# Token lists in bf16 in the buffer of stored rows, two experts' weights loaded earlier, and another order of constants and fills, in a fused attention and mixture-of-experts kernel

## The chip, the cores and the metric

The kernel runs on one core of one Trainium2 chip. The metric is the device time of one execution in microseconds (us); lower is better. In the text PE is the matrix engine (PEld its weight loads), DVE the vector engine, ACT the scalar engine, POOL the GpSimd engine, and SP the engine that issues most DMAs.

## The reference

```
x = x + layernorm(attn(layernorm(x)))        # x: (4, 1024, 256) f32
x = x + layernorm(ffn(layernorm(x)))

attn(c):  Q, K, V = c@Wq, c@Wk, c@Wv         # 16 heads of 16
          alpha = softmax(Q K^T / 4)         # over all keys
          alpha = where(causal, alpha, 0)    # masked after the softmax
          return alpha @ V

ffn(x):   probs = softmax(x @ router_w)      # 8 experts
          w, idx = top_k(probs, 2); w /= sum(w)
          return sum over e of combine[:, e] * (gelu(x @ w_fc[e]) @ w_proj[e])   # 256 -> 1024 -> 256
```

## The kernel before

The program goes through four stages, each engine with an instruction stream of its own, written out by hand. Semaphores alone order the engines.

**Stage 1, about 0 to 118 us.** Eight chunks of 512 tokens are normalised (DVE), transposed (PE, L931) and projected to Q, K and V (PE, L943 and L952). Q and K are split in three bf16 parts and stored to DRAM. Before it, POOL writes all constants. PE transposes with the constant `ident`, which is finished at L646 behind all fills; ACT's square root for the first chunk (L790) stands behind a warm-up activation (L786) that reads `cst0`, a constant that POOL fills at L627. Three of the fills, at L623, put ones into rows 96 to 119 of the three slots `ks` that hold K: each is 24 partitions by 4096 bf16 elements.

**Stage 2, about 118 to 1008 us.** Attention in 16 groups of four heads.

**Stage 3, about 1008 to 1057 us: routing.** Tokens are in eight blocks `g` of four tiles of 128, taken in the order `ORDER` = 0, 1, 2, 3, 4, 5, 7, 6; step `i` handles block `ORDER[i]`. The normalised rows lie in `yx`. SP stores them to DRAM (`store_x2`, L560; semaphore `s_x2w[i]`), so that rows can be gathered for each expert later, and stores the two gates of each token (`store_gate`, L565). `choose(i)` (DVE) picks the two best experts, `count(i)` (PE) ranks the tokens of each expert, `place(i)` (DVE) computes each token's slot. `place` also writes into `yx` a one-hot list `lo1` of the slot within a tile (L1310), for which the rows there must have been stored; it waits for `s_x2w[i]`. The last two steps, `i` = 6 and 7, come after the attention is over.

Then DVE, ACT and PE invert the map from tokens to slots. There are 64 (token tile, choice) pairs, handled in 4 batches of 16, with two buffers `hi1` in `arena`. For each batch, `hot` (L1522) compares the column `colf` of each pair with 71 numbers (`iota_c`), `hot_v` (L1529) multiplies the result with a value `vtab`, ACT (L880) multiplies it with the partition number, and PE (L1130) runs 16 matmuls of 142 moving columns that add everything up in one bank. `hot` of batch q waits for PE's batch q-2. From the sums DVE makes `tok` (L1549 to L1555), the list of rows to gather.

**Stage 4, about 1057 to 1625 us.** 71 tiles of 128 token slots, each of one expert: gather (POOL, L751), transpose (PE, L1142), first product (L1153), gelu (ACT), second product (L1163), scale (DVE), scatter with addition (POOL, L759). DVE copies the expert's first weights to `w1` (`copy_w`, L1560). The second weights lie in `arena`, whose part for experts 4 and 5 holds `hi1` during stage 3: SP loads these two (L553) once the lists are done and the first two gathers have landed, then it stores `x1` to the output (L600). PE waits for all second weights (`s_wp`) between the first product of tile 0 and that of tile 1. At the end the sums are normalised and added to the output.

Of the kernel before, what the change touches and what calls it, by code (L numbers as in the profile page):

```python
# [5 lines left out]
def sandwich(nc, x_d, wq_d, wk_d, wv_d, router_d, wfc_d, wproj_d, out_d):  # L6
# [7 lines left out]
    P = 128  # L14
# [33 lines left out]
    with ctx:  # L48
# [3 lines left out]
        def sem(name):  # L52
# [21 lines left out]
        lo1 = yx[:, :, :].rearrange("p t d -> p (t d)").bitcast(BF16).rearrange("p (g w) -> p g w", g=TT // TPC)\  # L74
            [:, :, 0:TOPK * TPC * P].rearrange("p g (j t l) -> p g j t l", j=TOPK, l=P)
# [4 lines left out]
        assert HSL * HW3 <= 2 * WSTEP and NPR % PCE == 0  # L80
# [78 lines left out]
        vtab = sb("vtab", [P, TOPK, TT])  # L159
# [6 lines left out]
        colf = rt[:, 0:TOPK * TT].rearrange("p (j t) -> p j t", j=TOPK)  # L166
# [39 lines left out]
        s_const = sem("s_const")  # L206
        s_x = [sem("s_x0"), sem("s_x1")]
# [63 lines left out]
        s_lc = sem("s_lc")  # L271
        s_hi = sem("s_hi")
# [176 lines left out]
        NCONST = 26  # L449
# [33 lines left out]
        def _(sp):  # L483
# [100 lines left out]
            for c in range(4 * KC, 6 * KC):  # L584
                load_wfc(c)
            for i in range(6):
                store_gate(i)
            for i in range(6, G):
                store_x2(i)
            for i in range(6, G):  # L590
                store_gate(i)
            sp.wait_ge(s_inv, NPR // PCE)
            for s in range(2):
                sp.wait_ge(s_xs[s], 16)
            for e in (4, 5):
                load_wproj(e)
# [13 lines left out]
        def _(pool):  # L610
            pool.memset(ident[:, :], 0.0).then_inc(s_const, 1)
            pool.memset(lower[:, :], 1.0).then_inc(s_const, 1)
# [8 lines left out]
            pool.wait_ge(s_const, 8 + NSL)  # L621
            for u in range(NSL):
                pool.memset(ks[u][MROW:MROW + MR], 1.0).then_inc(s_const, 1)  # L623
            pool.wait_ge(s_const, 8 + 2 * NSL)
            pool.memset(vone[:, 0:DH], 0.0).then_inc(s_const, 1)
            pool.memset(vone[:, DH:VW], 1.0).then_inc(s_const, 1)
            pool.memset(cst0[:, :], 0.0).then_inc(s_zero, 1)  # L627
# [18 lines left out]
            pool.affine_select(out=ident[:, :], in_=ident[:, :], compare_op=ALU.not_equal, fill=1.0,  # L646
                               base=0, pattern=[[-1, P]], channel_multiplier=1).then_inc(s_ident, 1)
# [136 lines left out]
        def _(act):  # L784
# [137 lines left out]
        def _(pe):  # L922
# [188 lines left out]
            pe.wait_ge(s_const, NCONST)  # L1111
            groups(pe, body)
# [11 lines left out]
            for q in range(NPR // PCE):  # L1124
# [4 lines left out]
                for n in range(PCE):  # L1129
                    ins = nc.tensor.matmul(bk(7)[:, 0:2 * NT], lo1[:, (q * PCE + n) % TT // TPC, (q * PCE + n) // TT, (q * PCE + n) % TPC, :],  # L1130
                                           hi1[q % HSL][:, n, 0:2, :].rearrange("p v c -> p (v c)"),
                                           start=(q == 0 and n == 0), stop=(q * PCE + n == NPR - 1),
                                           skip_group_check=True)
# [24 lines left out]
            def second_product(t, s, off):  # L1158
                wait_pos(pe, s_yo, t - 1)
# [20 lines left out]
            pe.wait_ge(s_wp, 16 * E)  # L1180
# [12 lines left out]
        def _(dve):  # L1193
# [52 lines left out]

            stats_c(0, 0, 16)
# [39 lines left out]
            def place(i):  # L1287
# [19 lines left out]
                dve.wait_ge(s_x2w[i], 16)  # L1307
                dve.wait_ge(s_lo, 3 * i + 3)
                for j in range(TOPK):
                    ins = nc.vector.tensor_tensor(lo1[:, g, j, :, :], lof[:, j, tiles].unsqueeze(2).to_broadcast([P, TPC, P]),  # L1310
                                                  iota_l[:, :].unsqueeze(1).to_broadcast([P, TPC, P]), ALU.is_equal)
# [204 lines left out]
            colf_n = rt[:, 0:TOPK * TT]  # L1516
            vtab_n = vtab[:, :, :].rearrange("p j t -> p (j t)")

            def hot(q):

                wait_pos(dve, s_inv, q - HSL + 1)
                nc.vector.tensor_tensor(hi1[q % HSL][:, :, 2, :],  # L1522
                                        colf_n[:, q * PCE:(q + 1) * PCE].unsqueeze(2).to_broadcast([P, PCE, NT]),
                                        iota_c[:, :].unsqueeze(1).to_broadcast([P, PCE, NT]),
                                        ALU.is_equal).then_inc(s_hi, 1)

            def hot_v(q):
# [125 lines left out]
```

## Time and profile before

| | |
|---|---|
| time, median of 3 runs | 1622.24 us (1619.61, 1622.24, 1626.62) |
| the profiled execution: time | 1626.82 us |
| its span, first to last instruction | 1625.1 us |
| busy: PE, DVE, ACT, POOL | 90%, 63%, 47%, 38% |
| mean granted clock of PE | 0.946 |
| PE, first product of the experts (L1153) | 270.3 us busy, x2272 |
| DMA moved | 105.07 MB, mean 65 GB/s |

The span holds everything that an engine did; the profiled execution's own time is 1.7 us longer. A busy PE says little about where time could be won, because most of it are the matmuls of stages 2 and 4, which the change leaves alone. What matters here are two short stretches in which PE stands still or works in fits: the first 18 us and the stretch from about 1000 to 1074 us.

### The profile page before, as it was taken

How to read it: one execution, taken by the hardware profiler on the slowest of the kernel's cores; microseconds unless marked ns; L12 is line 12 of the kernel's file. 1: busy time of each engine (PE TensorE's matmuls, PEld its weight loads, DVE VectorE, ACT ScalarE, POOL GpSimd, SP SyncE). 2: the span in 40 equal slices, each digit the busy share in tenths (PEclk: the TensorE clock that was granted, in tenths of full speed). 3: DMA queues.
4: the chain of work that ended last, by engine and by line, in shares of the span. 5: the costliest groups of instructions: out<-in, count | busy, mean ns of one | idle time of the engine just before them, and what ended most of it. 6: DMA issues, size and time to landing. Idle time of an engine off the chain costs nothing.

```text
span 1625.1 us, 31177 instructions
## 1 busy us (share of the span) xinstructions
PE 1455.0 (90%) x9750; PEld 836.1 (51%) x9751; DVE 1026.3 (63%) x1770; ACT 771.8 (47%) x1650; POOL 612.1 (38%) x711
## 2 busy tenths in 40 slices
PE   5988999999999899989999986389999999999990
PEld 3551233333333233323333243289999999999980
DVE  4769777777888788878888977723323233233324
ACT  2330577777777677767777785211111111111114
POOL 5332334543444334533444432123333333333332
PEclk9995899999999999999999998589999999999995
DMA  3569122022220222022213153262222222222229
GB/s 113 172 164 276 40 40 40 10 31 40 40 40 8 35 40 40 15 27 40 40 23 70 53 182 142 45 183 34 39 33 38 39 33 39 34 37 39 32 30 210
DMA packets 87629, 105.07 MB, mean 65 GB/s; under 512 B 11648, under 2 KB 70912, under 8 KB 87520
## 3 DMA queue, kind: packets, MB, share of 16 engines
q1 hardware_dynamic: 69664, 80.80, 21.5%
q0 software_dynamic: 17856, 22.89, 8.9%
q8 instruction: 60, 0.98, 0.3%
q14 instruction: 49, 0.40, 0.1%
HBM read 64.70 MB, written 38.96 MB: 64 GB/s over the span
## 4 chain that ended last, share of the span: by engine, by line
PE 61%; DVE 15%; issue 13%; ACT 4%; POOL 3%; DMA 2%; DVEq 1%; SPq 0%; POOLq 0%; ACTq 0%
PE ps L1153 16%; PE ps L1163 15%; PE ps L1008 10%; DVE negmax L1443 9%; PE ps L980 8%; PE ps L1094 8%; ACT wfc L868 2%; POOL x L668 2%; PE ps L973 2%; PE ps L1081 1%; DVE x L1348 1%; PE ps L1142 1%; ACT wfc L911 1%; DVE wfc L1454 1%; DMA arena<-in_L_ffn_w_proj 1%
## 5 line engine op out<-in xcount | busy, mean ns | idle before, releaser
L1443 DVE TENSOR_REDUCE negmax<-ps 128x1 f32<-128x1024 f32 x512 | 605.9, 1216 | 123.8 <-PE ps L1094 121.3
L868 ACT ACTIVATE wfc<-ps 128x512 f32<-128x512 f32 x768 | 436.6, 595 | 171.2 <-PE ps L980 162.7
L889 ACT ACTIVATE yx<-ps 128x512 f32<-128x512 f32 x142 | 84.8, 597 | 440.6 <-PE ps L1153 440.6
L1153 PE MATMUL ps<-yx 128*128 128x128 f32 x2272 | 270.3, 278 | 4.1 <-DMA arena<-in_L_ffn_w_proj 3.4
L1153 PEld LDWEIGHTS ps<-yx 128*128 128x128 f32 x2272 | 269.7, 195 | 8.3 <-DMA arena<-in_L_ffn_w_proj 3.6
L1163 PE MATMUL ps<-arena,yx 128*128 x1136 | 256.8, 379 | 0.0
L731 POOL TENSOR_TENSOR wfc<-wfc,causal 128x512 f32<-128x512 f32 x128 | 162.6, 1270 | 249.6 <-ACT wfc L868 181.7
L1094 PE MATMUL ps<-arena 96*128 96x512 bf16 x704 | 231.5, 413 | 9.6 <-DVE negmax L1443 4.0
L759 POOL DMA_INDIRECT expert_out<-yx,rt x71 | 112.6, 1586 | 318.3 <-DVE yx L1576 315.3
L1163 PEld LDWEIGHTS ps<-arena,yx 128*128 128x128 f32 x1136 | 210.4, 190 | 25.7
L980 PE MATMUL ps<-arena 120*128 120x512 bf16 x528 | 203.3, 392 | 12.8 <-ACT wfc L868 0.4
L1564 DVE SCALAR_TENSOR_TENSOR rt<-yx,rt 128x1 f32 (+1 forms) x71 | 15.6, 219 | 233.7 <-PE ps L1142 233.7
L1008 PE MATMUL ps<-wfc 128*16 128x128 f32 (+4 forms) x2304 | 161.5, 382 | 0.1
L863 ACT ACTIVATE ps<-ps 128x512 f32<-128x512 f32 x256 | 149.6, 584 | 11.7 <-PE ps L973 3.7
L980 PEld LDWEIGHTS ps<-arena 120*128 120x128 bf16 x528 | 50.2, 97 | 184.9 <-ACT wfc L868 115.0
L1560 DVE COPY yx<-wfc 128x2048 f32 x71 | 87.1, 1227 | 37.9 <-issue 37.9
L1094 PEld LDWEIGHTS ps<-arena 96*128 96x128 bf16 x704 | 65.5, 101 | 78.6 <-DVE negmax L1443 42.2
L1008 PE MATMUL ps<-wfc,vone 128*17 128x128 f32 (+3 forms) x1024 | 95.6, 445 | 7.2 <-issue 6.4
L1008 PEld LDWEIGHTS ps<-wfc 128*17 128x17 f32 (+1 forms) x2304 | 60.4, 97 | 76.1 <-issue 51.7
L980 PE MATMUL ps<-wfc 120*128 120x512 bf16 x240 | 93.0, 388 | 7.1 <-ACT wfc L868 0.8
L698 POOL TENSOR_TENSOR mparts<-negmax,zero 128x8 bf16<-128x8 f32 x64 | 12.8, 200 | 225.7 <-DVE negmax L1443 134.5
L751 POOL DMA_INDIRECT yx<-expert_in,rt x71 | 72.0, 1014 | 63.9 <-DVE rt L1555 34.8
(177 smaller groups left out, 1364.7 us busy)
## 6 DMA issues: line engine op xcount, KB each, us to landing
arena<-qk_parts SPq DMA_DIRECT2D x132, 128.0 KB, 5.9
qk_parts<-x SPq DMA_DIRECT2D x32, 384.0 KB, 2.6
arena<-in_L_ffn_w_proj SPq DMA_DIRECT2D x8, 1024.0 KB, 8.6
wfc<-in_L_ffn_w_fc SPq DMA_DIRECT2D x16, 512.0 KB, 7.5
wfc<-qk_parts SPq DMA_DIRECT2D x60, 128.0 KB, 6.1
expert_out<-rt SPq DMA_DIRECT2D x3, 1408.0 KB, 12.0
yx<-in_L_attn_content SPq DMA_DIRECT2D x8, 512.0 KB, 3.9
x<-in_L_attn_content SPq DMA_DIRECT2D x1, 4096.0 KB, 25.5
```

Of the source, the lines that this page charges most:

```text
L731: pool.tensor_tensor(md_sb[b % NET], et_sb[b % NET][:, :, q:q + P], causal[:, :].unsqueeze(1).to_broadcast([P, GH, P]), ALU.mult).then_inc ...
L759: pool.indirect_dma_start(out=ys_d, in_=yslot[t % 2], in_offset=None, out_offset=bass.IndirectOffsetOnAxis(ap=tok[:, t:t + 1], axis=0), co ...
L863: nc.scalar.activation(bk(ebank(c, g)), bk(ebank(c, g)), ACT.Exp, accum_out=den_u[:, (u - back) % NSL, hl, i:i + 1]).then_inc(s_expB, 1)
L868: nc.scalar.activation(et_sb[b % NET][:, hl, :], bk(ebank(c, g)), ACT.Exp).then_inc(s_expB, 1)
L889: nc.scalar.activation(hidT[s][:, 4 * hf:4 * hf + 4, :], bk(1 + hf).rearrange("p (c t) -> p c t", c=4), ACT.Gelu).then_inc(s_ge, 1)
L980: nc.tensor.matmul(bk(ebank(c, g)), ks[v][0:MROW + MR, hl, i * P:(i + 1) * P], qs[v][0:MROW + MR, hl, hf * 512:(hf + 1) * 512], start=True ...
L1008: ins = nc.tensor.matmul(out[32 * hl:32 * hl + rows, q0:q1], lhs, rhs, start=(i == 0 and piece == 0 and n == 0), stop=False, skip_group_ch ...
L1094: ins = nc.tensor.matmul(bk(2 * (k % 2) + hf), qs[u][0:SROWS, hl, i * P:(i + 1) * P], ks[u][0:SROWS, hl, hf * 512:(hf + 1) * 512], start=T ...
L1153: ins = nc.tensor.matmul(bk(1 + hf)[:, c * P:(c + 1) * P], w1[s][:, kc * FF + (4 * hf + c) * P:kc * FF + (4 * hf + c + 1) * P], xsT[:, kc, :],
L1163: ins = nc.tensor.matmul(bk(5 + s)[:, 0:D], hidT[s][:, c, :], arena[:, ds(off + c * D, D)], start=(c == 0), stop=(c == FC - 1))
L1443: nc.vector.tensor_reduce(negmax[:, hl % 2, i:i + 1], ps[:, 2 * (k % 2):2 * (k % 2) + 2, :], AX.XY, ALU.max, negate=True).then_inc(s_max, 1)
L1560: nc.vector.tensor_copy(w1[s], wfc[:, ds(off, WSTEP)]).then_inc(s_w1, 1)
```

## The change

The change has four parts.

1. The lists. `lo1` is packed into the first half of `yx` (step `i` writes token tiles 2i and 2i+1, and waits for `s_x2w[i // 2]`); the two buffers `hi1` move from `arena` into the second half of `yx`, with a new constant `iota_cn` behind them, a bf16 table that POOL writes once the block there has been stored and transposed. `colf` and `vtab` become bf16, and the layout of a `hi1` buffer goes from (pair, variant, column) to (variant, column, pair). So all operands of `hot` and `hot_v` are bf16 with 16 neighbouring elements, and a PE matmul of the inversion reads its 142 columns 16 elements (32 bytes) apart. `hot` now waits for the stores of blocks in steps 4 to 7.
2. SP stores block 7 (step 6) ahead of the gates, loads the second weights of experts 4 and 5 directly behind it, and stores block 6 (step 7) between the gates.
3. PE waits for the second weights at the second product of tile 0, not ahead of the first product of tile 1.
4. The constants. POOL fills `cst0` and `ident` first and finishes `ident` at once. The three fills of `ks` go from POOL to DVE, ahead of its first instruction of stage 1, with a semaphore `s_ones` of their own.

```
-        lo1 = yx[...].rearrange("p (g w) -> p g w", g=TT // TPC)[:, :, 0:TOPK * TPC * P].rearrange("p g (j t l) -> ...")
-        hi1 = [arena[:, 4 * WSTEP + s * HW3:4 * WSTEP + (s + 1) * HW3].bitcast(BF16)
-               .rearrange("p (n v c) -> p n v c", v=3, c=NT) for s in range(HSL)]
+        yx_b = yx[:, :, :].rearrange("p t d -> p (t d)").bitcast(BF16)
+        LO1 = TOPK * TT * P
+        lo1 = yx_b[:, 0:LO1].rearrange("p (i j t l) -> p i j t l", i=TT // TPC, j=TOPK, l=P)
+        hi1 = [yx_b[:, LO1 + 2 * s * HW3:LO1 + 2 * (s + 1) * HW3].rearrange("p (v c n) -> p v c n", v=3, c=NT)
+               for s in range(HSL)]
+        iota_cn = yx_b[:, LO1 + 2 * HSL * HW3:LO1 + 2 * HSL * HW3 + NT * PCE].rearrange("p (c n) -> p c n", c=NT)
-        vtab = sb("vtab", [P, TOPK, TT])
+        vtab = sb("vtab", [P, TOPK, TT], BF16)
-        colf = rt[:, 0:TOPK * TT].rearrange("p (j t) -> p j t", j=TOPK)
+        colf = rt[:, 0:TOPK * TT // 2].bitcast(BF16).rearrange("p (j t) -> p j t", j=TOPK)
...
 SP
             for c in range(4 * KC, 6 * KC):
                 load_wfc(c)
+            store_x2(6)
+            for e in (4, 5):
+                load_wproj(e)
             for i in range(6):
                 store_gate(i)
-            for i in range(6, G):
-                store_x2(i)
+            store_x2(7)
             for i in range(6, G):
                 store_gate(i)
-            sp.wait_ge(s_inv, NPR // PCE)
-            for s in range(2):
-                sp.wait_ge(s_xs[s], 16)
-            for e in (4, 5):
-                load_wproj(e)
...
 POOL
+            pool.memset(cst0[:, :], 0.0).then_inc(s_zero, 1)
             pool.memset(ident[:, :], 0.0).then_inc(s_const, 1)
+            pool.wait_ge(s_const, 1)
+            pool.affine_select(out=ident[:, :], ...).then_inc(s_ident, 1)
...
-            for u in range(NSL):
-                pool.memset(ks[u][MROW:MROW + MR], 1.0).then_inc(s_const, 1)
...
+            pool.wait_ge(s_x2w[ORDER.index(G - 1)], 16)
+            pool.wait_ge(s_x2t, KC * (ORDER.index(G - 1) + 1))
+            pool.iota(iota_cn, [[P, NT], [0, PCE]], base=0, channel_multiplier=0,
+                      allow_small_or_imprecise_dtypes=True).then_inc(s_cn, 1)
...
 PE
-                                           hi1[q % HSL][:, n, 0:2, :].rearrange("p v c -> p (v c)"),
+                                           hi1[q % HSL][:, 0:2, :, n],
...
             def second_product(t, s, off):
+                if isinstance(t, int) and t == 0:
+                    pe.wait_ge(s_wp, 16 * E)
...
             step(0, 0, first=True)
-            pe.wait_ge(s_wp, 16 * E)
...
 DVE
+            for u in range(NSL):
+                nc.vector.memset(ks[u][MROW:MROW + MR], 1.0).then_inc(s_ones, 1)
             stats_c(0, 0, 16)
...
-                dve.wait_ge(s_x2w[i], 16)
+                dve.wait_ge(s_x2w[i // 2], 16)
...
             def hot(q):
+                if q < HSL:
+                    for i in ((4, 5), (6, 7))[q]:
+                        dve.wait_ge(s_x2w[i], 16)
+                if q == 0:
+                    dve.wait_ge(s_cn, 1)
                 wait_pos(dve, s_inv, q - HSL + 1)
-                nc.vector.tensor_tensor(hi1[q % HSL][:, :, 2, :],
-                                        colf_n[:, q * PCE:(q + 1) * PCE].unsqueeze(2).to_broadcast([P, PCE, NT]),
-                                        iota_c[:, :].unsqueeze(1).to_broadcast([P, PCE, NT]),
-                                        ALU.is_equal).then_inc(s_hi, 1)
+                nc.vector.tensor_tensor(hi1[q % HSL][:, 2],
+                                        colf_n[:, q * PCE:(q + 1) * PCE].unsqueeze(1).to_broadcast([P, NT, PCE]),
+                                        iota_cn, ALU.is_equal).then_inc(s_hi, 1)
```

In the order listings below the line numbers are those of each kernel's own text.

SP, the DMAs at the end of the attention and in stage 3; `in_L_ffn_w_fc` are the first weights, `in_L_ffn_w_proj` the second, `expert_in<-yx` the stored rows, `expert_in<-gate` the gates. Before:

```order
95 L542 DMA wfc<-in_L_ffn_w_fc 128x1024 x12
96 L565 DMA expert_in<-gate 128x4x2 x6
97 L560 DMA expert_in<-yx 128x4x256 x2
98 L565 DMA expert_in<-gate 128x4x2 x2
99 L553 DMA arena<-in_L_ffn_w_proj 128x8x256 x2
```

And after:

```order
95 L546 DMA wfc<-in_L_ffn_w_fc 128x1024 x12
96 L564 DMA expert_in<-yx 128x4x256
97 L557 DMA arena<-in_L_ffn_w_proj 128x8x256 x2
98 L569 DMA expert_in<-gate 128x4x2 x6
99 L564 DMA expert_in<-yx 128x4x256
100 L569 DMA expert_in<-gate 128x4x2 x2
```

One store of rows and the two weight loads moved ahead of the first six gates; the other store stayed behind them.

DVE, the start of the program. Before:

```order
1 L1192 UNCONDITIONAL_BRANCH
2 L1197 BN_STATS stats<-yx 128x6 x4
3 L1199 MEMSET pause 128x1
4 L1201 BN_AGGR mv<-stats 128x2 x4
5 L1203 TENSOR_SCALAR mv<-mv 128x4
```

And after; the fills named `arena` and `wfc` are the rows of ones of the three slots `ks`:

```order
1 L1197 UNCONDITIONAL_BRANCH
2 L1253 MEMSET arena 24x4096 x2
3 L1253 MEMSET wfc 24x4096
4 L1202 BN_STATS stats<-yx 128x6 x4
5 L1204 MEMSET pause 128x1
```

The three fills now stand ahead of the first statistics.

## Rows read from the trace of the kernel before

**Rows 1.** Timeline, 0 to 18 us: start, duration, instruction, idle time before it.
```profile
0.82 0.20 POOL L611 MEMSET ident<- 128x128 f32 x1 [0.29 <-POOLq L1642]
...
3.26 6.99 POOL L623 MEMSET arena<- 24x4096 bf16 x2
...
4.78 1.41 DVE L1197 BATCH_NORM_STATS2 stats<-yx 128x6 f32<-128x256 f32 x4 [4.64 <-DMA yx<-in_L_attn_content]
...
6.63 0.17 DVE L1203 TENSOR_SCALAR mv<-mv 128x4 f32<-128x4 f32 x1
...
13.98 0.20 ACT L786 ACTIVATE warm<-cst 128x1 f32<-128x1 f32 x1 [11.88 <-POOL mhalf L628]
14.09 0.19 ACT L790 ACTIVATE std<-mv 128x4 f32<-128x4 f32 x1
...
15.52 0.29 POOL L646 TENSOR_SCALAR_AFFINE_SELECT ident<-ident 128x128 f32<-128x128 f32 x1 [0.16 <-POOL iota_c L643]
...
16.10 1.94 PE L931 MATMUL ps<-ident,yx 128*128 128x128 f32 x8 [16.10 <-DVE yx L1209]
```

**Rows 2.** Timeline of DVE around its fill of 512 elements.
```profile
932.87 2.35 DVE L1443 TENSOR_REDUCE negmax<-ps 128x1 f32<-128x1024 f32 x2
935.40 0.48 DVE L1421 MEMSET ps<- 128x512 f32 x1 [0.18 <-DVE negmax L1443]
935.79 1.34 DVE L1326 BATCH_NORM_STATS2 stats<-yx 128x6 f32<-128x256 f32 x4
```

**Rows 3.** Timeline of DVE, 1010 to 1011 us: first parts of one `var_y`.
```profile
1010.50 0.18 DVE L1335 BATCH_NORM_AGGREGATE mv<-stats 128x2 f32<-128x6 f32 x1
1010.52 0.06 DVE L1333 MEMSET pause<- 128x1 f32 x1
```

**Rows 4.** Timeline of DVE, stage 3.
```profile
1020.19 0.17 DVE L1304 CAST lof<-loi 128x8 f32<-128x8 int32 x1
1025.20 1.29 DVE L1310 TENSOR_TENSOR yx<-lof,iota_l 128x512 bf16<-128x512 f32 x2 [4.83 <-DMA expert_in<-yx]
...
1026.90 0.18 DVE L1263 COPY rt<-ps 128x32 f32<-128x32 f32 x1
...
1036.01 2.59 DVE L1522 TENSOR_TENSOR arena<-rt,iota_c 128x1136 bf16<-128x1136 f32 x2
1038.52 2.59 DVE L1529 TENSOR_TENSOR arena<-arena,vtab 128x1136 bf16<-128x1136 bf16 x2
...
1049.45 0.23 DVE L1549 TENSOR_SCALAR rt<-ps 128x71 f32<-128x71 f32 x1 [0.85 <-PE ps L1130]
```

**Rows 5.** Timeline of PE, stage 3 and the first tiles of stage 4.
```profile
1023.50 0.61 PE L1048 MATMUL ps<-ident,rt 128*128 128x32 f32 x2 [0.48 <-ACT rt L836]
...
1040.00 3.94 PE L1130 MATMUL ps<-arena,yx 128*128 128x142 bf16 x32 [10.72 <-ACT arena L880]
...
1057.56 6.21 PE L1153 MATMUL ps<-yx 128*128 128x128 f32 x32 [0.74 <-DVE yx L1568]
...
1067.37 6.43 PE L1153 MATMUL ps<-yx 128*128 128x128 f32 x32 [3.38 <-DMA arena<-in_L_ffn_w_proj]
...
1077.31 3.73 PE L1153 MATMUL ps<-yx 128*128 128x128 f32 x32
```

**Rows 6.** Timeline of ACT, the lists.
```profile
1037.38 2.51 ACT L880 ACTIVATE arena<-arena,pcol 128x1136 bf16<-128x1136 bf16 x2 [8.91 <-DVE arena L1522]
```

**Rows 7.** Timeline of DVE, `copy_w` for tile 1.
```profile
1065.20 1.23 DVE L1560 COPY yx<-wfc 128x2048 f32 x1 [0.61 <-issue]
```

**Rows 8.** Timeline of SP, the issues ahead of the last stores.
```profile
1008.15 11.01 SPq L565 DMA_DIRECT2D expert_in<-gate  x6
1019.20 1.05 SPq L560 DMA_DIRECT2D expert_in<-yx  x2
...
1057.32 1.00 SPq L553 DMA_DIRECT2D arena<-in_L_ffn_w_proj  x2
```

**Rows 9.** Busy time by stretch: each engine, PE clock, DMA share, GB/s.
```profile
1066.00:1067.00 1.00, 0.00 (x0) 0.00 (x0) 0.42 (x1) 0.00 (x0) 0.54 (x1) 0.51 1.08 383
```

More of the change, by code:

```diff
@@ L73, in sandwich @@
         NPR = TOPK * TT
-        lo1 = yx[:, :, :].rearrange("p t d -> p (t d)").bitcast(BF16).rearrange("p (g w) -> p g w", g=TT // TPC)\
-            [:, :, 0:TOPK * TPC * P].rearrange("p g (j t l) -> p g j t l", j=TOPK, l=P)
         PCE, HSL = 16, 2
         HW3 = PCE * 3 * NT // 2
-        hi1 = [arena[:, 4 * WSTEP + s * HW3:4 * WSTEP + (s + 1) * HW3].bitcast(BF16)
-               .rearrange("p (n v c) -> p n v c", v=3, c=NT) for s in range(HSL)]
-        assert HSL * HW3 <= 2 * WSTEP and NPR % PCE == 0
+        yx_b = yx[:, :, :].rearrange("p t d -> p (t d)").bitcast(BF16)
[4 more added lines that the diff above has]
+        iota_cn = yx_b[:, LO1 + 2 * HSL * HW3:LO1 + 2 * HSL * HW3 + NT * PCE].rearrange("p (c n) -> p c n", c=NT)
+        assert LO1 + 2 * HSL * HW3 + NT * PCE <= 2 * TT * D and NPR % PCE == 0
         NET = 3
@@ L206, in sandwich @@
         s_const = sem("s_const")
+        s_ones = sem("s_ones")
         s_x = [sem("s_x0"), sem("s_x1")]
@@ L271, in sandwich @@
         s_lc = sem("s_lc")
+        s_cn = sem("s_cn")
         s_hi = sem("s_hi")
@@ L448, in sandwich @@
         CRT, CRP = 5, 2
-        NCONST = 26
+        NCONST = 23
         NZERO = 7
@@ L610, in _ @@
         def _(pool):
+            pool.memset(cst0[:, :], 0.0).then_inc(s_zero, 1)
             pool.memset(ident[:, :], 0.0).then_inc(s_const, 1)
+            pool.wait_ge(s_const, 1)
+            pool.affine_select(out=ident[:, :], in_=ident[:, :], compare_op=ALU.not_equal, fill=1.0,
+                               base=0, pattern=[[-1, P]], channel_multiplier=1).then_inc(s_ident, 1)
             pool.memset(lower[:, :], 1.0).then_inc(s_const, 1)
@@ L645, in _ @@
             pool.wait_ge(s_const, NCONST - 6)
-            pool.affine_select(out=ident[:, :], in_=ident[:, :], compare_op=ALU.not_equal, fill=1.0,
-                               base=0, pattern=[[-1, P]], channel_multiplier=1).then_inc(s_ident, 1)
             pool.affine_select(out=lower[:, :], in_=lower[:, :], compare_op=ALU.is_gt, fill=0.0,
@@ L879, in _ @@
                 act.wait_ge(s_hi, q + 1)
-                nc.scalar.activation(hi1[q % HSL][:, :, 0, :], hi1[q % HSL][:, :, 2, :], ACT.Copy,
+                nc.scalar.activation(hi1[q % HSL][:, 0], hi1[q % HSL][:, 2], ACT.Copy,
                                      scale=pcol[:, 0:1]).then_inc(s_hip, 1)
@@ L1111, in _ @@
             pe.wait_ge(s_const, NCONST)
+            pe.wait_ge(s_ones, NSL)
             groups(pe, body)
@@ L1129, in _ @@
                 for n in range(PCE):
-                    ins = nc.tensor.matmul(bk(7)[:, 0:2 * NT], lo1[:, (q * PCE + n) % TT // TPC, (q * PCE + n) // TT, (q * PCE + n) % TPC, :],
-                                           hi1[q % HSL][:, n, 0:2, :].rearrange("p v c -> p (v c)"),
+                    j, tt = divmod(q * PCE + n, TT)
+                    ins = nc.tensor.matmul(bk(7)[:, 0:2 * NT], lo1[:, ORDER.index(tt // TPC), j, tt % TPC, :],
+                                           hi1[q % HSL][:, 0:2, :, n],
                                            start=(q == 0 and n == 0), stop=(q * PCE + n == NPR - 1),
@@ L1306, in place @@
                     dve.wait_ge(s_zero, NZERO)
-                dve.wait_ge(s_x2w[i], 16)
+                dve.wait_ge(s_x2w[i // 2], 16)
                 dve.wait_ge(s_lo, 3 * i + 3)
                 for j in range(TOPK):
-                    ins = nc.vector.tensor_tensor(lo1[:, g, j, :, :], lof[:, j, tiles].unsqueeze(2).to_broadcast([P, TPC, P]),
+                    ins = nc.vector.tensor_tensor(lo1[:, i, j, :, :], lof[:, j, tiles].unsqueeze(2).to_broadcast([P, TPC, P]),
                                                   iota_l[:, :].unsqueeze(1).to_broadcast([P, TPC, P]), ALU.is_equal)
```

12 lines of the change are left out of this document (4 added, 8 removed).

## The prediction

> **What bounds the kernel now.** I read the share of busy time first, then the chain that ended last, then the timelines of the stretches that the change touches. For most of the span PE works without a pause, in attention and in the 71 expert tiles, and no edit reaches those matmuls. So the change can only move what stands in front of them: the start, the routing, and the hand-over to the first tiles.
>
> At the start PE begins at 16.10 us [rows 1]. Two things arrive together: the normalised rows (DVE L1209, the releaser named) and `ident`, whose last step runs at 15.52. The rows are late because ACT could only start at 13.98, after 11.88 us of waiting for a constant that POOL fills behind the fills of ones: the two in `arena` alone take 6.99 us, 3.5 each, and the third is alike. DVE had its variances at 6.63 + 0.17 = 6.80 and then stood still.
>
> In the routing DVE is the last to arrive almost everywhere. It waits 4.83 us for a store to land, from about 1020.4 to 1025.20, then works through to the lists, which take from 1036.01 to 1049.45 [rows 4]. In stage 4 PE waits 3.38 us at 1067.37 for the last second weights [rows 5].
>
> **1. The start.** POOL's three fills (10.5 us) leave the path; three DVE fills of 4096 elements come onto it, since the first statistics stand behind them in the same queue. The trace has no fill of SBUF of this size on DVE. Its nearest row has 512 elements: 0.48 us by its own duration, 0.39 us from its start to the next instruction's start at 935.79, and 0.57 us from the end of the instruction in front (932.87 + 2.35 = 935.22) [rows 2]. The start of such a row seems to be stamped late: the fill L1333 is issued ahead of all the L1335 and yet stands at 1010.52, behind the first of them at 1010.50 [rows 3]. So I take 0.57 less some 0.04 for the handing over, 0.53 us for 512 elements, or 1.04 ns each: 4.25 us for 4096, 12.8 for three. By 0.39 it would be 3.1 each and 9.4 in all; by 0.57, 13.7.
>
> The Trainium skill (VectorE: DVE Perf Modes, section Zero memsets can be issued as uint32 (trn2)) says that a memset takes one cycle per element whatever the type, so bf16 would not help here; by its clock of 0.96 GHz that is 12.8 us too. It is a rule against this edit.
>
> DVE can begin at about 0.8 us, as POOL does (0.82), so the fills end at 13.6. Then come 6.80 - 4.78 = 2.02 us of statistics, about 0.1 to ACT, and 16.10 - 14.09 = 2.01 us from ACT's root to PE: 17.8 against 16.10. `ident` and `cst0` are long ready, and POOL is free before its first task. **Term: +1.7 us** (13.7 us of fills: +2.6; 9.4: -1.7). If the fills took no time, the rows would be at hand at 4.78 and PE would start at 4.78 + 2.02 + 0.1 + 2.01 = 8.9: -7.2, the floor. Everything behind, up to the routing, shifts by the same.
>
> **2. The wait in step 6.** `place(6)` now waits for the store of step 3, long landed, so its list starts at about 1020.5 rather than 1025.20. But 4.7 us are not won: next is `choose(7)`, before at 1026.90, and it needs PE's logits, 1023.50 + 0.61 = 1024.11 [rows 4, 5]. PE's chain up to there doesn't depend on the removed wait. DVE is free at about 1022.2 and now waits for PE until 1024.2. **Term: 1026.90 - 1024.2 = -2.7 us.** What is late next is PE.
>
> **3. The lists.** Before, from the first `hot` to the use of the sums: 1049.45 - 1036.01 = 13.44 us. Two `hot` take 2.59 us, 1.34 each with 0.09 overlapping, and `hot_v` the same; two of ACT's copies 2.51; 32 matmuls 3.94, so 1.97 a batch and 123 ns a matmul [rows 4 to 6]. New: `hot` and `hot_v` with all operands bf16. The trace shows no such DVE instruction with two inputs; bounds are 1.34 (nothing gained) and, by the rate of L1560, 1.23 us for 2048 elements or 0.60 ns each [rows 7], 0.68. I take 0.75, near the latter: the operands now are as narrow and as regular as they can be. ACT's copy stays at 1.25, the number of elements is the same. PE's batch stays at 1.97, see below. From the new `hot` at 0: `hot` 0 ends at 0.75, `hot` 1 at 1.4, `hot_v` 0 at 2.05; ACT's first copy ends at 2.05, its second at 3.3. PE runs batch 0 from 2.2 to 4.2 and batch 1 to 6.1. `hot` 2 waits for batch 0 and ends at 5.1, ACT at 6.4; batch 2 runs from 6.5 to 8.5. `hot` 3 waits for batch 1, ends at 7.1, ACT at 8.4; batch 3 to 10.5; with 0.1 for the step to DVE 10.6. **Term: 10.6 - 13.4 = -2.8 us.** It isn't more because ACT and PE, not DVE, carry this chain now. Without any gain on DVE the term is 0.
>
> The new waits of `hot`: `s_cn` follows the store of step 6, which now is in front of the gates, and a table that POOL writes while idle; it is there by about 1023. The store of step 7 is issued behind six gates (11.01 us in all, from 1008.15 [rows 8]) and behind 2 MB of weights. Before, both stores had landed by about 1026. The weights add between 5.5 us (2.1 MB at the 383 GB/s of [rows 9]) and 10 (issued at 1057.32, landed at 1067.37 [rows 8, 5]): 1031.5 to 1036. `hot` 1 needs it at 1036.01 - 2.7 + 0.65 = 1033.95. Value 0, at worst +2. The stores of `x1` to the output, which now follow at once, are done before the first gather.
>
> **4. The second weights.** PE's wait of 3.38 us ends at 1067.37, but the first product of tile 1 also needs `copy_w`, which ends at 1065.20 + 1.23 = 1066.43 [rows 5, 7], and nothing here makes that earlier. **Term: 1066.5 - 1067.37 = -0.9 us.** What is late next is DVE's copy. The wait in its new place, at the second product, finds the weights there.
>
> **Reading 32 bytes apart.** No matmul of the trace reads its moving columns so. The nearest row that costs more per column is L1153: 128 f32 columns, 32 in 6.43 us, 201 ns or 1.57 ns a column against 0.87 for L1130 [rows 5]; at 1.57, 16 matmuls take 3.6 us and the lists 2.2 + 4 x 3.6 + 0.1 = 16.7, term +3.3 rather than -2.8. Value 1.97: PE's granted clock is at its lower level here (0.50 to 0.52), so that it asks for one column in 0.83 ns only. The Trainium skill (SBUF — State Buffer, section Door 1: The DMA port swizzle) says that SBUF works in lines of 16 bytes and that each access to a new line pays a penalty, up to a stride of 8 bf16 being free. Here every column would be a new line; it gives no price in time. By the rule the matmuls lengthen, and that is the third rival.
>
> **Sum.** +1.7 - 2.7 - 2.8 - 0.9 = -4.7 us. Against the profiled execution: 1626.8 - 4.7 = 1622.1. That execution is 4.6 us above the median of the runs (1622.24), as the same kernel's runs spread; so the median should be 1622.24 - 4.7 = **1617.5 us**.
>
> **The rivals.**
> - *Fast fills.* DVE fills bf16 in SBUF two or four elements a cycle: three in 6.4 or 3.2 us. PE starts at 11.4 or 8.9, the term is -4.7 or -7.2, the sum -11.1 to -13.6: 1608.6 to 1611.1. For it: DVE does 1.23 us for 2048 f32 in a copy [rows 7], so two a cycle exist. Against: the f32 row of [rows 2] shows one a cycle. Chance 0.18.
> - *The clock.* PE's first product of tile 1 took 6.43 us where a settled one takes 3.73 [rows 5]; the clock had fallen to its lower level by 1066.00 to 1067.00 (0.51) [rows 9], after PE had stood still since about 1064. It now starts at 1066.5 of that time, at the very edge. If the fall comes later it gains 2.7, and some 0.9 are in the last batch of the lists, as PE now pauses less between batches: sum about -8.3, 1613.9. Against: a pause of 2.5 us remains. Chance 0.14.
> - *The reading stride, the other side.* If a moving column 32 bytes from the last costs double, a batch takes 3.94 us, the lists 2.2 + 15.8 + 0.1 = 18.1, term +4.6, sum +2.7: 1624.9, slower. It decides from 202 ns a matmul (3.24 us a batch), where the term of the lists is +1.8 and the sum about 0. At 201 ns (the L1153 rate, or 1.6 x before) it just eats all. Chance 0.12.
> - *No gain from bf16 on DVE,* the change not doing what it says: the lists at 0, sum -1.9, 1620.3. Or the store of step 7 late by 2 us: 1619.5. Together 0.08.
> - The forecast: 0.48.
>
> **How the numbers follow.** A measurement of this kernel can tell some 0.5% (8.1 us) from no change, so faster means below 1614.1 and slower above 1630.4. Fast fills give faster nearly always (0.17); the clock case lies at the edge (0.08); from the forecast, with a shorter fill and the runs' own spread (7 us from lowest to highest), 0.07 more: 0.32. Slower: a stride that costs more than double, or a start or a store worse than bounded: 0.06. Same: 0.62. The range runs from 1608, which takes in nearly all of the fast fills, to 1625, the stride at double.
>
> **What the profile after would show.** The three fills on DVE from 0.8 us, and PE's first transpose at 17.8 (11.4 or 8.9 in the first rival). `choose(7)` waiting for PE, not for a DMA, at about 4.7 - 2.7 = 2 us. `hot` at 0.75 us. PE's batches of the lists in 1.97 us; at 3 or more the stride is to blame. From the first `hot` to L1559 10.6 us. PE's wait before tile 1 2.5 us, put down to DVE's copy. The forecast falls if fills run more than one element a cycle, if a `hot` still takes 1.34, or if the first product of a settled tile (3.73 us) changes at all.

## The result, and the profile after

The changed kernel takes 1627.73 us (median of 20 runs, 1625.10 to 1630.22) where the kernel before, on the same chip, takes 1623.72 (20 runs, 1619.61 to 1626.62). The ratio is 1.0024, 95% interval 1.0018 to 1.0031: 4.0 us slower (2.9 to 5.0 by the interval). I had forecast 1617.5, between 1608 and 1625. The forecast was wrong: a gain of 4.7 us turned into a loss of 4.0.

The profiled execution of the changed kernel took 1627.36 us, with a span of 1625.6 and a mean granted clock of 0.946. That of before had the same clock and a span of 1625.1, because it was one of the longer runs of its kernel (1626.8 against a median of 1623.7). So the two spans hide most of the difference, and stages are compared by their own length.

The start, as the timeline of the changed kernel shows it (start, duration, instruction, idle time before it):

```profile
1.73 3.47 DVE L1253 MEMSET arena<- 24x4096 bf16 x1 [1.58 <-PEq L1652]
6.00 3.47 DVE L1253 MEMSET arena<- 24x4096 bf16 x1 [0.80 <-issue]
10.27 3.47 DVE L1253 MEMSET wfc<- 24x4096 bf16 x1 [0.80 <-issue]
13.78 1.41 DVE L1202 BATCH_NORM_STATS2 stats<-yx 128x6 f32<-128x256 f32 x4
...
16.29 1.38 DVE L1214 TENSOR_SCALAR yx<-yx,mv,rstd 128x256 f32<-128x256 f32 x4
...
17.82 1.94 PE L933 MATMUL ps<-ident,yx 128*128 128x128 f32 x8 [17.82 <-DVE yx L1214]
```

From one fill's start to the next's are 4.27 us, though a row says 3.47: the missing 0.80 stands as "issue" in front of the next row. It fits the late start stamp that [rows 2, 3] hinted at, and the fills of half as many elements below bear it out. PE starts at 17.82 instead of 16.10 [rows 1]: +1.72, forecast +1.7.

Stage 3 on DVE, the timeline of the changed kernel. The stage begins at 1008.95 here and at 1009.05 before, so these times can be held against [rows 4] nearly as they are:

```profile
1020.73 1.29 DVE L1317 TENSOR_TENSOR yx<-lof,iota_l 128x512 bf16<-128x512 f32 x2 [0.46 <-DVE lof L1311]
...
1024.04 0.19 DVE L1270 COPY rt<-ps 128x32 f32<-128x32 f32 x1 [1.05 <-PE ps L1050]
...
1033.17 1.41 DVE L1534 TENSOR_TENSOR yx<-rt,yx 128x1136 bf16<-128x1136 bf16 x2
1034.50 1.41 DVE L1540 TENSOR_TENSOR yx<-yx,vtab 128x1136 bf16<-128x1136 bf16 x2
...
1039.77 0.75 DVE L1534 TENSOR_TENSOR yx<-rt,yx 128x1136 bf16<-128x1136 bf16 x1 [3.22 <-PE ps L1134]
...
1043.80 0.75 DVE L1534 TENSOR_TENSOR yx<-rt,yx 128x1136 bf16<-128x1136 bf16 x1 [2.50 <-PE ps L1134]
...
1052.02 0.23 DVE L1559 TENSOR_SCALAR rt<-ps 128x71 f32<-128x71 f32 x1 [5.60 <-PE ps L1134]
```

The wait for the store has gone: `place(6)` starts at 1020.73, and `choose(7)` waits for PE's logits and starts at 1024.04 instead of 1026.90, after 1.05 us of waiting for them (I had put this wait at 2). A `hot` takes 0.75 us instead of 1.34. But from then on DVE waits for PE again and again, 3.22, 2.50 and 5.60 us. The reason stands on PE, in its timeline of the changed kernel:

```profile
1023.40 0.60 PE L1050 MATMUL ps<-ident,rt 128*128 128x32 f32 x2 [0.47 <-ACT rt L838]
...
1035.39 16.60 PE L1134 MATMUL ps<-yx 128*128 128x142 bf16 x64 [8.94 <-DVE yx L1540]
...
1060.15 6.36 PE L1157 MATMUL ps<-yx 128*128 128x128 f32 x32 [0.74 <-DVE yx L1578]
...
1068.79 5.47 PE L1157 MATMUL ps<-yx 128*128 128x128 f32 x32 [2.06 <-DVE yx L1570]
...
1077.77 3.73 PE L1157 MATMUL ps<-yx 128*128 128x128 f32 x32
```

All 64 matmuls stand in one unbroken group of 16.60 us: 259 ns each, against 123 ns [rows 5]. PE never waits there any more, it is the bound. From the first `hot` to the use of the sums are 1052.02 - 1033.17 = 18.85 us, before 13.44. The second weights did move as meant: PE's wait ahead of tile 1 is now put down to DVE's copy and is 2.06 us instead of 3.38.

### The profile page after: what moved, and what is told of

It is laid out like the page before. It is cut to its first block, busy times and chain, and to the rows that moved or that the text cites. A ratio compares the mean times of both kernels' runs of the same rounds, so it can differ in the third digit from the quotient of the medians.

```text
span 1625.6 us, 31180 instructions
## 1 busy us (share of the span) xinstructions
PE 1459.6 (90%) x9750; PEld 835.8 (51%) x9751; DVE 1036.4 (64%) x1773; ACT 771.6 (47%) x1650; POOL 603.2 (37%) x709
## 4 chain that ended last, share of the span: by engine, by line
PE 62%; DVE 15%; issue 13%; ACT 4%; POOL 3%; DMA 1%; DVEq 1%; SPq 0%; POOLq 0%; ACTq 0%
PE ps L1157 16%; PE ps L1169 15%; PE ps L1010 10%; DVE negmax L1450 9%; PE ps L982 8%; PE ps L1096 7%; ACT wfc L870 2%; POOL x L666 2%; PE ps L975 2%; PE ps L1134 1%; DVE x L1355 1%; PE ps L1083 1%; PE ps L1146 1%; ACT wfc L913 1%; DVE wfc L1461 1%
## 5 line engine op out<-in xcount | busy, mean ns | idle before, releaser
L1586 DVE TENSOR_SCALAR yx<-ps,rt 128x256 f32<-128x256 f32 x71 | 34.3, 484 | 98.4 <-PE ps L1169 98.4
L696 POOL TENSOR_TENSOR mparts<-negmax,zero 128x8 bf16<-128x8 f32 x64 | 12.8, 200 | 226.1 <-DVE negmax L1450 134.8
```

## The experiments

Theory A, after the result: the moving columns of L1134, read at a stride of 32 bytes, make each matmul 136 ns longer and the lists 5.4 us longer; all other parts do what the forecast said. Theory B: something else slows these matmuls (the buffers that moved from `arena` to `yx`, the stores to the output beside them, or the low clock). A second question was whether the start could be had without DVE's 12.8 us.

Each kernel was timed against the kernel before on the same chip; "before" below is the median of those runs of it. Where two changed kernels are compared, each is first taken against its own "before". The profile rows of a section are from the kernel of its heading unless another is named.

### Only the stride added to the kernel before

```
-  .rearrange("p (n v c) -> p n v c", v=3, c=NT)     # columns of one n are neighbours
+  .rearrange("p (v c n) -> p v c n", v=3, c=NT)     # 32 bytes apart; buffers stay in arena, tables f32
```

> The kernel before with one edit: the order of elements in the list buffers is (variant, column, pair), the buffers stay in arena, colf and vtab stay f32, no DMA runs beside the lists. Theory A (the stride alone): a matmul takes 259 ns instead of 123, four batches 16.6 us on PE, the lists 20.7 us instead of 13.4 since the first batch starts as late as before; 7.3 us slower than the kernel before, about 1631 us (ratio 1.0045). Theory B (yx, bf16 or the DMAs beside): 123 ns, no difference.

Measured: 1631.54 us (before 1623.32), ratio 1.0053 (1.0039 to 1.0066). The timeline:

```profile
1032.13 2.59 DVE L1522 TENSOR_TENSOR arena<-rt,iota_c 128x1136 bf16<-128x1136 f32 x2
...
1036.12 16.60 PE L1130 MATMUL ps<-arena,yx 128*128 128x142 bf16 x64 [10.71 <-ACT arena L880]
...
1052.76 0.23 DVE L1549 TENSOR_SCALAR rt<-ps 128x71 f32<-128x71 f32 x1 [4.42 <-PE ps L1130]
```

The window over the lists (length, busy time of PE, PEld, DVE, ACT and POOL, then PE clock, DMA share and GB/s), and behind it one from the kernel before, at its own first batch:

```profile
1036.00:1053.00 17.00, 16.60 (x64) 7.94 (x64) 8.49 (x10) 3.98 (x5) 0.00 (x0) 0.50 0.00 0
```

```profile
1040.00:1041.00 1.00, 1.00 (x9) 1.00 (x10) 1.00 (x1) 0.00 (x0) 0.00 (x0) 0.50 0.00 0
```

The group has 16.60 us again, to the hundredth, with the buffers in `arena`, f32 tables and no DMA running (0 GB/s). The first `hot` stands at 1032.13, so the lists take 20.63 us, 7.2 more than before. This one edit costs 8.2 us. Theory A is shown, and B falls: of its three causes two are absent here, and the third, the low clock, is there with neighbouring columns too (0.50 in both windows), so it does not slow a matmul by itself. Whether the stride would cost anything at the higher clock is not shown.

### The changed kernel with the old order

```
-  hi1: .rearrange("p (v c n) -> p v c n")   hot, hot_v: [P, NT, PCE]   PE: hi1[..][:, 0:2, :, n]
+  hi1: .rearrange("p (n v c) -> p n v c")   hot, hot_v: [P, PCE, NT]   PE: hi1[..][:, n, 0:2, :]
   # hot reads the f32 constant iota_c again; POOL's table iota_cn and the wait for it are dropped
```

> The changed kernel with the old order of elements in the list buffers (pair, variant, column), so that a matmul of the inversion reads its 142 columns side by side; the buffers stay in yx and everything else stays as changed. Theory A (the stride: columns 32 bytes apart slow the moving reads): the 64 matmuls fall from 259 ns to some 123 ns each, a hot takes 1.34 us again, the lists take 13.4 us from the first hot to the use of the sums instead of 18.85; 5.4 us less than the changed kernel, about 1622.3 us, and about 2 us below the kernel before (ratio 0.9988). Theory B (what slows the matmuls is where and when they run: operands in yx, or the 4 MB of output stores that now run beside them): the matmuls stay at about 259 ns and the time at about 1627.7 us or more.

Measured: 1619.85 us (1619.11 to 1622.02; before 1623.03), ratio 0.998 (0.9971 to 0.9989). From its timeline, PE and then DVE:

```profile
1036.90 3.94 PE L1129 MATMUL ps<-yx 128*128 128x142 bf16 x32 [10.71 <-ACT yx L877]
...
1054.67 5.54 PE L1152 MATMUL ps<-yx 128*128 128x128 f32 x32 [0.74 <-DVE yx L1572]
...
1062.48 3.84 PE L1152 MATMUL ps<-yx 128*128 128x128 f32 x32 [2.06 <-DVE yx L1564]
```

```profile
1032.90 2.59 DVE L1527 TENSOR_TENSOR yx<-rt,iota_c 128x1136 bf16<-128x1136 bf16 x2
...
1035.41 2.59 DVE L1534 TENSOR_TENSOR yx<-yx,vtab 128x1136 bf16<-128x1136 bf16 x2
...
1046.58 0.23 DVE L1553 TENSOR_SCALAR rt<-ps 128x71 f32<-128x71 f32 x1 [1.10 <-PE ps L1129]
```

The matmuls are back at 123 ns in `yx`, which takes the place of the buffers out of theory B as well. `hot` and `hot_v` are back at 1.33 to 1.35 us each. `hot` reads `iota_c`, which is f32, but every operand of `hot_v` (L1534) is bf16 and it gains nothing either: in this order its second input repeats one element 71 times at the innermost level. The other way round, `hot_v` of the kernel with only the stride added is regular but has an f32 table, and takes 1.34 us. So DVE's gain needs the narrow type and the regular order, and it is that order which makes PE step 32 bytes. The lists take 13.68 us, and the other parts of the change gain 0.2% by themselves. The time is 3.2 us below that of before (1.8 to 4.7), so 7.2 below the changed kernel's. By the profiles the lists account for 5.2 of it, and the first products of the first two tiles, 5.54 and 3.84 us against 6.36 and 5.47, for another 2.5. Those two come from the clock: in the first tile it rose earlier, and ahead of the second it did not fall. Two windows of this kernel, over the pause ahead of the second tile's product, and in a fence of its own two of the changed kernel:

```profile
1061.00:1062.00 1.00, 0.00 (x0) 0.00 (x0) 0.82 (x2) 0.00 (x0) 0.71 (x1) 1.00 0.00 0
1062.00:1063.00 1.00, 0.52 (x4) 0.52 (x5) 0.43 (x1) 0.00 (x0) 1.00 (x1) 1.00 0.00 0
```

```profile
1068.00:1069.00 1.00, 0.21 (x1) 0.21 (x2) 0.73 (x1) 0.00 (x0) 1.00 (x1) 0.96 0.00 0
1069.00:1070.00 1.00, 1.00 (x6) 1.00 (x6) 0.00 (x0) 0.00 (x0) 0.55 (x1) 0.50 0.00 0
```

The pause is 2.06 us in both. Why the clock fell in the one and not in the other is open.

### How far apart is too far

```
-  PCE, HSL = 16, 2
+  PCE, HSL = 8, 2      # columns 16 bytes apart, 8 batches     (second kernel: 4, 2: 8 bytes, 16 batches)
   # POOL writes its table iota_cn only behind the stores of steps 4 to 7
```

> The changed kernel with batches of 8 pairs: the columns of a matmul lie 16 bytes apart instead of 32. If each column in a new 16-byte line costs the same, a matmul stays at 259 ns; if the cost grows with the distance, it falls to some 190 ns.

> The changed kernel with batches of 4 pairs: columns 8 bytes apart, two of them in each 16 bytes. If two hits per 16-byte line are enough for the full rate, a matmul takes 123 ns; if any distance above neighbouring costs, 259 ns or between.

Measured, one run each, so that the rows say more than the times: 1629.36 us at 16 bytes and 1619.91 at 8. The timeline at 16 bytes, then two batches of four matmuls at 8:

```profile
1037.82 16.32 PE L1135 MATMUL ps<-yx 128*128 128x142 bf16 x64 [9.07 <-ACT yx L883]
```

```profile
1039.34 1.24 PE L1135 MATMUL ps<-yx 128*128 128x142 bf16 x8 [0.40 <-ACT yx L883]
```

At 16 bytes a matmul takes 255 ns, as at 32. At 8 bytes the four matmuls of a batch start 0.11 to 0.13 us apart, about as with neighbouring columns (0.12). So the step lies between 8 and 16 bytes, and from 16 to 32 bytes the price hardly grows. Only powers of two were tried, so a step by 16-byte lines is not told apart here from another cause that sets in at a stride of 16. The Trainium skill (SBUF — State Buffer, section Door 1: The DMA port swizzle) says two things on this: that a line has 16 bytes and wants at least two hits to run at full rate, with which the three groups agree (two hits a line at 8 bytes, one at 16 and 32), and that a stride of 8 bf16 is still free, with which they don't: that is the 16-byte case, and it costs the whole 132 ns here, 0.93 ns for each of the 142 columns.

### Both wishes at once: pairs

DVE wants bf16 operands that are regular at the innermost level, PE wants neighbouring columns. Two copies of each table entry side by side serve both:

```
+  hi1  [n, v, 72]                        # order as before, one column of padding
+  colf [j, t, 2], vtab [j, t, 2]         # every value stored twice
+  hot: in0 = colf_n[:, q*16:(q+1)*16, :].unsqueeze(2).to_broadcast([P, 16, 36, 2]), in1 = iota_cb (bf16)
```

> The changed kernel with the list buffers in the order (pair, variant, column) and 72 columns, and with colf and vtab stored twice side by side, so that DVE still sees neighbouring bf16 elements in all operands and PE still reads neighbouring columns. Theory A: hot 0.75 us, matmuls 123 ns, the lists 10.6 us as first forecast; 8 us below the changed kernel, about 1619.5 us, 4 to 5 us below the kernel before (ratio 0.997). Theory B: matmuls at 259 ns, 1627.7 us. If an innermost run of two elements isn't enough for the fast rate of DVE, hot takes 1.35 us and the time is that of rows_layout, 1622 us.

Measured: 1616.88 us (1616.46 to 1618.84; before 1623.03), ratio 0.9959 (0.9946 to 0.9972): 6.2 us below the kernel before. From its timeline:

```profile
1034.64 1.43 DVE L1538 TENSOR_TENSOR yx<-rt,iota_cb 128x1152 bf16<-128x1152 bf16 x2
...
1036.88 3.53 PE L1133 MATMUL ps<-yx 128*128 128x142 bf16 x32 [9.02 <-DVE yx L1545]
...
1043.81 0.23 DVE L1563 TENSOR_SCALAR rt<-ps 128x71 f32<-128x71 f32 x1 [0.68 <-PE ps L1133]
```

A `hot` takes 0.76 us and the matmuls stay short: the lists take 9.17 us, 1.4 less than the 10.6 that the forecast gave for a short `hot` with short matmuls. Part of it is the clock, granted at its higher level from about 1040 here, as two windows of this kernel show (columns as above), and, in a fence of its own, one of the changed kernel in its lists:

```profile
1038.00:1040.00 2.00, 2.00 (x21) 2.00 (x20) 0.98 (x3) 0.17 (x1) 0.00 (x0) 0.55 1.05 357
1040.00:1042.00 2.00, 1.27 (x21) 1.08 (x19) 1.97 (x4) 1.79 (x2) 0.00 (x0) 1.00 1.04 341
```

```profile
1048.00:1052.00 4.00, 3.99 (x16) 1.72 (x14) 0.00 (x0) 0.00 (x0) 0.00 (x0) 0.50 0.00 0
```

In the changed kernel PE shows as busy for 16.6 us without a gap and the clock stays at 0.50, its lower level (1.2 GHz). In the pairs kernel PE even pauses, and the clock goes to 1.00.

### The start on its own

```
before + the part of the change that moves the fills of ones to DVE and the constants into another order; lists, stores, weights untouched
```

> The kernel before with only the new order of constants and fills (part 4 of the change). Forecast term: PE starts at 17.8 instead of 16.1 us and everything shifts: +1.7 us, about 1625 us, ratio 1.001. Rival (the attention gives it back): 0.

Measured: 1624.37 us (12 runs; before 1623.43), ratio 1.0009 (0.9999 to 1.002), PE starting at 17.82. In microseconds the interval runs from -0.2 to +3.2, so it takes in both 0 and the forecast +1.7, and this run decides nothing about how much of the start reaches the end. The kernels with shorter fills, below, do.

### The fills on POOL, behind the constants

```
   # end of POOL's constants
+  for u in range(NSL): pool.memset(ks[u][MROW:MROW + MR], 1.0).then_inc(s_ones, 1)
   # DVE
-  for u in range(NSL): nc.vector.memset(ks[u][MROW:MROW + MR], 1.0).then_inc(s_ones, 1)
```

> The changed kernel with the three fills of ones back on POOL, but behind all its constants. Theory A: nothing but DVE's statistics stands before the first transpose; PE starts at 8.9 us instead of 17.8, and this shifts everything: 8.9 us less than the changed kernel, about 1618.8 us (ratio to the kernel before 0.997). POOL is free at about 17.5 us, just as its first task comes, at worst some tenths late. Theory B (the attention stage gives back what the start loses or gains, as the profiled executions of the two kernels could suggest, which stand at the same time at 1009 us): less than 3 us of it shows in the time.

Measured: 1627.68 us, ratio 1.0027 (1.0016 to 1.0038): nothing gained, where about 9 us were expected. It says nothing on whether a start 9 us earlier would reach the end, since PE did not start earlier. From its timeline:

```profile
7.10 7.11 POOL L663 MEMSET arena<- 24x4096 bf16 x2
7.55 10.72 DVE L1218 TENSOR_SCALAR yx<-yx,mv,rstd 128x256 f32<-128x256 f32 x4
14.15 3.65 POOL L663 MEMSET wfc<- 24x4096 bf16 x1
...
18.42 1.94 PE L937 MATMUL ps<-ident,yx 128*128 128x128 f32 x8 [18.42 <-DVE yx L1218]
```

And the view of the tile that DVE writes there (shortest, median and longest in ns, first and last start):

```profile
L1218 DVE TENSOR_SCALAR yx<-yx,mv,rstd x4: 395/3442/3678, 7.6 to 17.9; 128x256 f32<-128x256 f32 x4
```

DVE has its statistics early, but its four normalising instructions take 10.72 us where four took 1.38 in the changed kernel. Three of them last about as long as a fill of POOL (7.11 / 2 = 3.56 and 3.65): the first, which starts 0.45 us behind the first fill, takes 3.21, the next two 3.68 each. The last, which starts at 17.9, after the third fill's end at 17.80, takes 0.395. The theory that POOL's fills are harmless off the path fell, and a new one took its place: while POOL runs one fill, DVE's L1218 waits for its end. If so, short fills should not hurt.

### The same fills in 48 short pieces

```
+  for c in range(16): pool.memset(flat[:, c * 256:(c + 1) * 256], 1.0).then_inc(s_ones, 1)   # per slot
```

> The changed kernel with the fills of ones on POOL behind its constants, as in fills_pool, but in 48 pieces of 256 elements instead of 3 of 4096. If DVE's four normalising instructions wait each for the POOL instruction that is running (in fills_pool they took 3.2 to 3.7 us each instead of 0.35), they now wait 0.3 us at most and PE starts at 9 to 11 us instead of 18.4: 7 to 9 us below the changed kernel, about 1619.5 us. If instead both engines share something by the byte, the four take as long as before, 10.7 us in all, and PE starts at 18.

Measured: 1618.15 us (before 1623.43), ratio 0.9967 (0.9956 to 0.9979): 9.3 us below the changed kernel, where PE's start explains 8.7.

```profile
7.10 8.76 POOL L666 MEMSET arena<- 24x256 bf16 x32
7.32 1.68 DVE L1221 TENSOR_SCALAR yx<-yx,mv,rstd 128x256 f32<-128x256 f32 x4
9.15 1.94 PE L940 MATMUL ps<-ident,yx 128*128 128x128 f32 x8 [9.15 <-DVE yx L1221]
```

The same bytes on the same engine at the same place, only cut up: POOL is at its fills all the while and is even slower with them (0.27 us for 256 elements), yet DVE takes 1.68 us instead of 10.72, and PE starts at 9.15 instead of 18.42. The waiting is for the whole instruction of the other engine, as the Trainium skill says (SBUF — State Buffer, section Who interferes with whom) of DVE in a mode that uses two ports and GpSimd: whoever starts first has the shared ports to the end of its instruction. That L1218 is in such a mode no row says; that it waits for whole instructions the two kernels together show. The changed kernel seems to have a small case of it as well: DVE's L1322, 0.16 us before, takes 0.64 there and ends at 1022.58, beside POOL's new table (1021.13 to 1022.56); in the two kernels without that table it is 0.16 again.

### The fills on DVE as 4-byte words

```
-  nc.vector.memset(ks[u][MROW:MROW + MR], 1.0)                                    # 4096 bf16
+  nc.vector.memset(slots[u][MROW:MROW + MR, GQK:2 * GQK], 1.0019378662109375)     # 2048 f32, whose two halves are bf16 1.0
```

> The changed kernel with each DVE fill written as 2048 f32 words, whose bits are two bf16 ones, instead of 4096 bf16 elements. If a fill takes one cycle per element whatever the type, each takes 2.13 us instead of 4.27, PE starts at about 11.4 us instead of 17.8: 6.4 us less than the changed kernel, about 1621.3 us. If it goes by bytes, no difference. The rows of these fills should read 1.74 us (0.83 ns per element plus 0.06), less than they occupy.

Measured: 1620.94 us (before 1623.32), ratio 0.9983 (0.9974 to 0.9992), 6.4 below the changed kernel.

```profile
1.30 1.76 DVE L1253 MEMSET arena<- 24x2048 f32 x1 [1.16 <-PEq L1652]
3.44 1.76 DVE L1253 MEMSET arena<- 24x2048 f32 x1 [0.38 <-issue]
...
11.42 1.94 PE L933 MATMUL ps<-ident,yx 128*128 128x128 f32 x8 [11.42 <-DVE yx L1214]
```

Half the elements take half the time: 2.14 us from start to start, 1.04 ns an element as before, whatever its width. The first row ends at 1.30 + 1.76 = 3.06 here and at 5.20 in the changed kernel; less 2.14 and 4.27 us, both fills begin at about 0.93. So it is the start of such a row that is late. PE starts 6.40 us earlier, and all of it reaches the end.

### Pairs with the fills on POOL, and the best of all

> Both: the lists in pairs and the fills on POOL behind the constants. Theory A: the two gains add up, 8.2 + 8.9 = 17 us less than the changed kernel, about 1610.6 us, 13 us below the kernel before (ratio 0.992). Theory B for the start: about 1619 us.

The pairs kernel with POOL's long fills behind the constants: 1614.97 us, ratio 0.9948 (0.9933 to 0.9962), 4 us more than expected. POOL's fills again hold DVE up (L1217, four in 7.93 us), and PE starts at 15.40.

```
   # pairs, and on DVE
+  for u in range(2): fill(u)     # as 4-byte words, ahead of the first statistics
   ...                            # DVE's loop of stage 1
+  fill(2)                        # the third, used last, behind it
```

> The lists in pairs, and the fills of ones on DVE as f32 words (2.13 us each): two of them ahead of the first statistics, where DVE waits for its input anyway, the third behind its last work of stage 1, where it waits for ACT. Theory (the two faults of the change are the reading stride and what stands ahead of DVE's first normalised rows): PE starts at 9.2 us, the lists take 9.2 to 10.6 us; against the kernel before, -6.9 for the start, -2.8 for the wait, -2.8 to -4.3 for the lists, -0.9 for the weights: 13.4 to 14.9 us less, about 1609 us, ratio 0.991. Rival: the start isn't carried through to the end, as with fills_pool; then as pairs, 0.996.

Measured: **1607.72 us** (1604.76 to 1610.26; before 1623.43), ratio 0.9904 (0.9891 to 0.9917). From its timeline:

```profile
9.28 1.94 PE L932 MATMUL ps<-ident,yx 128*128 128x128 f32 x8 [9.28 <-DVE yx L1213]
...
1023.49 1.43 DVE L1541 TENSOR_TENSOR yx<-rt,iota_cb 128x1152 bf16<-128x1152 bf16 x2
...
1033.03 0.23 DVE L1566 TENSOR_SCALAR rt<-ps 128x71 f32<-128x71 f32 x1 [0.69 <-PE ps L1133]
```

PE starts at 9.28 and the lists take 1033.03 - 1023.49 = 9.54 us. It beats both kernels, by 15.7 us the one before.

## Why the prediction was wrong

**Reading 32 bytes apart: the step that failed.** The forecast put a batch at "Value 1.97", because "PE's granted clock is at its lower level here (0.50 to 0.52), so that it asks for one column in 0.83 ns only". A batch took 16.60 / 4 = 4.15 us. The stride alone on the kernel before reproduces it, and the stride removed takes it away. The argument had no row behind it: at the lower clock neighbouring columns take 0.87 ns, strided ones 1.82. That PE asks slowly does not say what the memory can give. The mechanism stood in the prediction as the third rival, with 3.94 us a batch and 1624.9 us in all, at a chance of 0.12. It was even dearer than that. The nearest dearer row, L1153 with 1.57 ns a column, was put in as a bound and then left for the value that cost nothing. Its weight was also misread later on: at 1.57 ns a column a matmul of 142 columns takes 223 ns and the sum is -1.9 + 3.3 = +1.4, a loss, while the list of rivals takes 201 ns, which is for 128 columns, and says that this rate "just eats all".

**3. The lists.** Forecast -2.8 us, measured +5.4 (13.44 to 18.85). The DVE part was right: `hot` in 0.75 us, as taken. By the prediction's own reckoning with 4.15 us a batch, 2.2 + 16.6 + 0.1 = 18.9, so nothing but that one number was missing. The pairs kernel shows the other half: the lists at 9.2 to 9.5 us once DVE's gain comes without PE's loss.

**1. The start.** Forecast +1.7, measured +1.72, with the price of a fill at 4.27 us (forecast 4.25). The estimate by the stamp that comes late held; the first rival, fast fills, did not occur.

**2. The wait in step 6.** Forecast -2.7; `choose(7)` starts 2.86 us earlier by the two profiles, 2.76 by the distance from the beginning of stage 3. What was named as next, PE's logits, is what it waits for. Its wait for them is 1.05 us, not 2. Shown in the traces only: this part was not run alone.

**4. The second weights.** Forecast -0.9. From the use of the sums to the first product of tile 1 are 1068.79 - 1052.02 = 16.77 us, before 17.92: -1.15. This too was not run alone. The first product itself is 5.47 us instead of 6.43, another -0.96, which comes from the clock.

**The new waits.** Costed at 0: the two pairs of `hot` and `hot_v` follow one another without a gap (1033.17 and 1034.50), so the store of step 7 and POOL's table (written by 1022.56) were there in time.

**The sum.** The terms as measured, +1.7 - 2.8 + 5.4 - 1.15, make +3.2 us; with the clock in tile 1 +2.2. Measured are +4.0 (2.9 to 5.0). The 0.8 to 1.8 us that remain are open. They do not lie behind the start of stage 3: from there to the end of the span are 616.65 us in the changed kernel and 616.05 before, +0.6, and the terms of that part with the clock in tile 1 make +0.5. They are smaller than what the stretch from PE's first transpose to that of stage 3 moves by itself: in the profiles of the thirteen kernels it lasts between 989.8 and 993.5 us, and it is 1.8 us shorter in the changed kernel's than in that of before. The changed kernel with the old order checks the other three terms together: it measures -3.2 us (-4.7 to -1.8), where the forecast had -1.9 for them. 1.5 us of the distance between forecast and result are nothing of the change: the three runs shown at first had a median of 1622.24, the twenty beside the result 1623.72.

**The clock.** The second rival came true in part. Before, the clock had fallen ahead of tile 1's first product; after the change that product starts at 1068.79, just ahead of the fall, and is 0.96 us shorter, not 2.7. The 0.9 us in the lists did not come, the clock stayed at 0.50 there. That the earlier start of the product is the reason is not shown: with the same pause of 2.06 us the clock did not fall at all in the kernel with the old order, where the product takes 3.84.

## What to carry to other kernels

When a layout is turned to please one engine, look at what every other reader of that buffer now steps over; a matmul's moving operand wants neighbouring columns, and two per 16 bytes were enough here. A bound taken from a dearer row must not be dropped for an argument that no row bears out, above all where one term of the sum hangs on it four times over. And often both engines can be served: storing small tables twice side by side gave the gain without its price.

## What the runs showed of the hardware

- A bf16 matmul of 142 moving columns at the lower clock takes 123 ns with neighbouring columns, about 130 ns at 8 bytes apart (one run), 255 at 16 (one run) and 259 at 32. Whether the step is there at the higher clock was not tried.
- The row of a long fill on DVE hides a fifth of it: 4096 elements read 3.47 us, and the next start comes after 4.27. The cost follows the number of elements, not their width (2048 words of 4 bytes: 2.14 us).
- A fill on POOL of 3.6 us holds up an f32 tensor-scalar instruction on DVE for its whole length (four of them, 1.38 us of work, took 10.72 beside three fills); beside pieces of 256 elements they took 1.68.
- A DVE instruction with two bf16 inputs, one of them repeated over a middle dimension with a run of only two elements at the innermost level, takes 0.76 us for 1152 elements; with one f32 input 1136 take 1.34.
- A PE that shows as busy without a gap for 16.6 us may still be left at 1.2 GHz (0.50 throughout).
